# Last stage of a fused encoder: turning the normalised rows with transposing transfers on SyncE's queue instead of with TensorE

## The reference, cut to what matters

```python
h = einsum('bhid,oi,od->bho', x, weighted_sum, weight)      # mixing stage
h = concatenate([h, txt], axis=1)                           # 8 x 589 rows of 256
h = h + attn(layernorm(h))                                  # attention over the 8 rows of a position
h = h + ffn(layernorm(h))                                   # the last stage

def ffn(x):                                                 # x is layernorm(h)
    hn = rmsnorm(x, gamma1)                                 # "the normalised rows"
    q = hn @ Wq + bq
    kv = (hn @ Wdown + bdown) @ Wup + bup
    att = softmax(q k^T / 4) over the 16 heads of one row
    x = x + (att v) @ Wo + bo
    h2 = rmsnorm(x, gamma2)
    gate = softmax(h2 @ Wg + bg)                            # 8 experts
    return x + sum_e gate_e * (h2 @ We[e])
```

## Time and profile before

| | |
|---|---|
| median of 3 runs | 833.88 us (833.34 to 834.82) |
| profiled execution | 829.93 us, span 828.1 us |
| TensorE (PE) | 769.2 us busy, 93% |
| VectorE (DVE) | 729.4 us busy, 88% |
| ScalarE (ACT) | 335.1 us busy, 40% |
| GpSimd (POOL) | 405.2 us busy, 49% |
| mean granted clock of TensorE | 0.987 |

### The profile page before, as it was taken

The page is one execution under the profiler, slowest core; times in us unless marked ns, Lnnn a source line. Parts: engine busy times, 40 slices in busy tenths (PEclk is TensorE's granted clock), DMA queues, the critical chain, the costliest instruction groups (busy, mean ns, idle before and its releaser), DMA issues.

```text
span 828.1 us, 48492 instructions
## 1 busy us (share of the span) xinstructions
PE 769.2 (93%) x20348; PEld 512.0 (62%) x20348; DVE 729.4 (88%) x1702; ACT 335.1 (40%) x874; POOL 405.2 (49%) x1129
## 2 busy tenths in 40 slices
PE   4999978998998888986999999999999999999998
PEld 3888755665666666655666666666666656665654
DVE  5799678999999999975899999999999999999996
ACT  4577434444444444433333333333333333333321
POOL 1231355666665666743554455445545554554321
PEclk9999999999999999987999999999999999999999
DMA  9986000000000000000000000000000000000000
GB/s 329 340 213 217 1 3 4 1 0 0 0 0 0 0 0 0 4 4 4 11 10 15 13 13 6 13 13 13 6 13 13 13 6 13 13 6 13 14 16 19
DMA packets 17064, 28.38 MB, mean 34 GB/s; under 512 B 3474, under 2 KB 12258, under 8 KB 17002
## 3 DMA queue, kind: packets, MB, share of 16 engines
q1 hardware_dynamic: 17002, 27.49, 10.3%
HBM read 22.64 MB, written 4.83 MB: 33 GB/s over the span
## 4 chain that ended last, share of the span: by engine, by line
PE 62%; DVE 15%; issue 5%; ACT 3%; POOL 2%; DVEq 0%; ACTq 0%; POOLq 0%
PE bank L204 15%; PE bank L206 12%; PE bank L205 12%; PE bank L935 6%; PE bank L946 6%; DVE ss L462 3%; PE bank L287 3%; POOL rt L496 2%; PE bank L962 2%; DVE on_t_l L408 2%; PE bank L1004 2%; PE bank L953 2%; DVE k_t L459 1%; DVE sc L426 1%; DVE pr_t L439 1%
## 5 line engine op out<-in xcount | busy, mean ns | idle before, releaser
L1099 DVE SCALAR_TENSOR_TENSOR acc<-bank,gate,acc 128x256 f32<-128x256 f32 x222 | 105.3, 474 | 8.9 <-PE bank L206 2.5
L204 PE MATMUL bank<-we_h,h_t_h 128*128 128x512 f16 x296 | 113.0, 382 | 0.1
L206 PE MATMUL bank<-we_h,h_t_l 128*128 128x512 f16 x296 | 112.2, 379 | 0.0
L205 PE MATMUL bank<-we_l,h_t_h 128*128 128x512 f16 x296 | 112.2, 379 | 0.0
L204 PE MATMUL bank<-tokw_h,x_t_h 128*128 128x256 f16 x256 | 70.6, 276 | 11.7 <-DVE x_t_l L673 11.7
L206 PE MATMUL bank<-tokw_h,x_t_l 128*128 128x256 f16 x256 | 70.5, 275 | 0.0
L205 PE MATMUL bank<-tokw_l,x_t_h 128*128 128x256 f16 x256 | 70.5, 275 | 0.0
L946 PEld LDWEIGHTS bank<-pr_t,v 32*32 32x32 f32 x4736 | 48.1, 106 | 31.6 <-issue 31.6
L496 POOL TENSOR_TENSOR rt<-rn 128x32 f32<-128x32 f32 x111 | 26.5, 238 | 75.0 <-DVE rn L473 69.1
L935 PEld LDWEIGHTS bank<-kv_t,fq_t 32*32 32x32 f32 x4736 | 48.1, 106 | 18.8 <-issue 18.8
L375 ACT ACTIVATE pr<-sc 128x512 f32<-128x512 f32 x37 | 23.3, 630 | 87.8 <-DVE sc L426 87.8
(11 more groups left out here) (218 smaller groups left out, 2214.0 us busy)
## 6 DMA issues: line engine op xcount, KB each, us to landing
xbuf<-in_x SPq DMA_DIRECT2D x32, 512.0 KB, 5.4
out<-res SPq DMA_DIRECT2D x36, 128.0 KB
we_s<-in_we SPq DMA_DIRECT2D x4, 512.0 KB, 6.4
inw<-in_in_w SPq DMA_DIRECT2D x1, 768.0 KB, 11.0
wrep<-in_w_rep SPq DMA_DIRECT2D x1, 512.0 KB, 4.7
h_all<-in_txt SPq DMA_DIRECT2D x1, 512.0 KB
wst<-in_wst_in SPq DMA_DIRECT2D x1, 256.0 KB, 2.7
outw<-in_out_w SPq DMA_DIRECT2D x1, 256.0 KB, 11.0
```

What stands on the lines that cost most here:

```text
L204: nc.tensor.matmul(dst, a_h(c), b_h(c), start=start and c == 0, stop=False)
L205: nc.tensor.matmul(dst, a_h(c), b_l(c), start=False, stop=False)
L206: last = nc.tensor.matmul(dst, a_l(c), b_h(c), start=False, stop=stop and c == chunks - 1)
L1099: op = nc.vector.scalar_tensor_tensor(out=(res if e == E - 1 else acc)[:, :], in0=b_we[s % 2][:, k * D:(k + 1) * D], scalar=gate[p][:, e:e ...
```

## The change: what it does

The two transposes on TensorE, the copy to `hn_h` on ScalarE and the subtraction on VectorE go. ScalarE now writes the rows twice as they lie: `hn` in fp32 and, with the same operation, `hn_r[0]` in fp16. GpSimd subtracts the one from the other and writes `hn_r[1]` in fp16; the operation stands first in its part of a turn. Two transposing transfers of 128x256 fp16 elements each (64 KB), issued by SyncE, write `hn_h` and `hn_l` as before. They wait for the subtraction (`p_hnl`) and for the last reader of the tile before (`f_down`). TensorE waits for both to have landed (`hn_in`) before it multiplies with `wq`; ScalarE waits for the same before it writes the next tile's rows, because the transfers read `hn_r`. SyncE's loop is written out, with the transfers of tile `i` ahead of the output of tile `i - 4`.

```diff
@@ -821,6 +821,7 @@
         hn_h, hn_l = halves("hn_t", [P, KC, P])
+        hn_r = halves("hn_r", [P, D])
@@ ffn_pe
                 if real(i, 1):
-                    pe.wait_ge(f_htl, i + 2)
+                    pe.wait_ge(hn_in, 32 * (i + 2))
                     wait(pe, f_logit, i - 1)
                     rows_times(b_q[:, 0:D], hn_h, hn_l, ...
...
-                if real(i, 2):
-                    pe.wait_ge(f_hn, i + 3)
-                    wait(pe, f_x2, i)
-                    for c in range(KC):
-                        last = nc.tensor.transpose(b_hn[:, c * P:(c + 1) * P], hn[:, c * P:(c + 1) * P], ident[:, :])
-                    last.then_inc(f_hnps, 1)
@@ ffn_act
-                if real(i, 2):
-                    act.wait_ge(f_hnps, i + 3)
-                    wait(act, f_down, i + 2)
-                    nc.scalar.activation(hn_h[:, :, :], b_hn[:, 0:D], ACT.Copy).then_inc(f_hth, 1)
                 if real(i, 3):
                     settle(act, ls_ready)
-                    wait(act, f_hnps, i + 3)
+                    wait(act, p_hnl, i + 3)
+                    wait(act, hn_in, 32 * (i + 3))
                     act.wait_ge(p_all, i + 4)
                     at = bass.ds(i + 3, 1)
-                    nc.scalar.activation(hn[:, :], h_all[:, at, :].squeeze(1), ACT.Identity,
-                                         bias=..., scale=...).then_inc(f_hn, 1)
+                    for rows in (hn, hn_r[0]):
+                        last = nc.scalar.activation(rows[:, :], h_all[:, at, :].squeeze(1), ACT.Identity,
+                                                    bias=..., scale=...)
+                    last.then_inc(f_hn, 1)
@@ ffn_dve
-                if real(i, 2):
-                    dve.wait_ge(f_hth, i + 3)
-                    nc.vector.tensor_tensor(hn_l[:, :, :], b_hn[:, 0:D], hn_h[:, :, :], ALU.subtract).then_inc(f_htl, 1)
@@ ffn_pool
             def body(i, p):
+                if real(i, 2):
+                    pool.wait_ge(f_hn, i + 3)
+                    nc.gpsimd.tensor_tensor(hn_r[1][:, :], hn[:, :], hn_r[0][:, :], ALU.subtract).then_inc(p_hnl, 1)
@@ block.sync
-                with sp.Fori(0, TILES - 1) as i:
-                    sp.wait_ge(f_comb, (i + 1) * STEPS)
-                    sp.dma_start(out[bass.ds(i * P, P), :], res[:, :]).then_inc(out_done, 16)
-                sp.wait_ge(f_comb, TILES * STEPS)
-                sp.dma_start(out[(TILES - 1) * P:TOKENS, :], res[0:TAIL, :]).then_inc(out_done, 16)
+                for i in range(TILES + 4):
+                    if i < TILES:
+                        sp.wait_ge(p_hnl, i + 1)
+                        wait(sp, f_down, i)
+                        sp.dma_start_transpose(hn_h[:, :, :], hn_r[0][:, :]).then_inc(hn_in, 16)
+                        sp.dma_start_transpose(hn_l[:, :, :], hn_r[1][:, :]).then_inc(hn_in, 16)
+                    if i >= 4:
+                        at = (i - 4) * P
+                        rows = min(P, TOKENS - at)
+                        sp.wait_ge(f_comb, (i - 3) * STEPS)
+                        sp.dma_start(out[at:at + rows, :], res[0:rows, :]).then_inc(out_done, 16)
```

More of the change, by code:

```diff
@@ L902, in ffn_coefficients @@
             nc.gpsimd.tensor_copy(cf_all[:, at, :], cf[:, :].unsqueeze(1)).then_inc(p_all, 1)
-        names = ("f_hn", "f_hnps", "f_hth", "f_htl", "f_q", "f_down", "f_lat", "f_qraw", "f_qpad", "f_kv", "f_kvt", "f_qt",
+        names = ("f_hn", "p_hnl", "hn_in", "f_q", "f_down", "f_lat", "f_qraw", "f_qpad", "f_kv", "f_kvt", "f_qt",
                  "f_s", "f_max", "f_sub", "f_exp", "f_prt", "f_av", "f_of", "f_rsum", "f_on", "f_onps", "f_onh", "f_onl",
@@ L910, in build @@
                  "f_gmul", "f_we", "f_comb", "f_acc", "f_x1", "p_x1", "p_hx2", "p_t2", "p_r2", "p_latl", "out_done")
-        (f_hn, f_hnps, f_hth, f_htl, f_q, f_down, f_lat, f_qraw, f_qpad, f_kv, f_kvt, f_qt,
+        (f_hn, p_hnl, hn_in, f_q, f_down, f_lat, f_qraw, f_qpad, f_kv, f_kvt, f_qt,
          f_s, f_max, f_sub, f_exp, f_prt, f_av, f_of, f_rsum, f_on, f_onps, f_onh, f_onl,
@@ L1061, in body @@
                     nc.scalar.activation(h2_t[1 - p][0][:, :, :], b_turn[:, 0:D], ACT.Copy).then_inc(f_h2h, 1)
-                if real(i, 2):
-                    act.wait_ge(f_hnps, i + 3)
-                    wait(act, f_down, i + 2)
-                    nc.scalar.activation(hn_h[:, :, :], b_hn[:, 0:D], ACT.Copy).then_inc(f_hth, 1)
                 if real(i, 3):
                     settle(act, ls_ready)
-                    wait(act, f_hnps, i + 3)
+                    wait(act, p_hnl, i + 3)
+                    wait(act, hn_in, 32 * (i + 3))
                     act.wait_ge(p_all, i + 4)
                     at = bass.ds(i + 3, 1)
-                    nc.scalar.activation(hn[:, :], h_all[:, at, :].squeeze(1), ACT.Identity,
-                                         bias=cf_all[:, at, NR:NR + 1].squeeze(1),
-                                         scale=cf_all[:, at, RR:RR + 1].squeeze(1)).then_inc(f_hn, 1)
+                    for rows in (hn, hn_r[0]):
+                        last = nc.scalar.activation(rows[:, :], h_all[:, at, :].squeeze(1), ACT.Identity,
+                                                    bias=cf_all[:, at, NR:NR + 1].squeeze(1),
+                                                    scale=cf_all[:, at, RR:RR + 1].squeeze(1))
+                    last.then_inc(f_hn, 1)
                 if real(i, -1):
```

## The result

| | before | after |
|---|---|---|
| median of the runs made together, us | 833.61 (830.86 to 834.82, 4 runs) | 842.83 (840.86 to 843.95, 4 runs) |
| profiled execution, us | 829.93 | 842.81 |
| its span, us | 828.1 | 841.0 |
| mean granted clock | 0.987 | 0.971 |

The ratio is 1.011, with a 95% interval of 1.0083 to 1.0138. The change costs about 9 us.

A forecast was written before the change was run, and what follows sets the result against it. A loop between VectorE (`smax` to `h_t_l`) and TensorE (gate to scores) sets the 11.9 us turn. 829.93 + 9.2 - 1.7 = 837.4 profiled; with 3.95 to the median, 841.4; 8-in-10 range 835 to 848.

The forecast's parts named there:

- Loop, 0: Last stage, turns 3 to 34: removed work only lengthens TensorE's and VectorE's waits, turns stay 11.9 us; gain 0.
- Rival B: Last stage's loop: the removed work does set the pace, so not slower, 824.0 us or 828.0 as median; chance 0.07.
- L, 4.3: SyncE's queue: time from issue of the pair's first transposing transfer to the second's landing, taken as 4.3 us from `wu_b`.
- The stall, 9.2: Head turn -2: ScalarE waits for tile 0's late subtraction and transfers, delaying body 35's exponential; all 9.2 us lost.
- Rival C: Seam of the stages: stall half taken up, 836.8 us, chance 0.05; or no stall at all, 832.2, chance 0.05.
- The head gives back, -1.7: Head turns -1 to 2: removed transposes and VectorE work leave the path, 0.57, 0.5 and twice 0.3 us, together -1.7.
- clock, 0: TensorE's clock behind the stall: already at 0.50 there, so 0 us, with bounds of -0.5 and +2.5.

The follow-up runs named there:

- experiment 5: Changed kernel with equal unread work put back in the old places, two transposes on TensorE and a subtraction on VectorE: 842.9 us, ratio 1.0089.
- experiments 8 and 9: VectorE writes `h_t_l` earlier, reciprocal and one expert's combine behind it: 8 on the changed kernel with subtraction-first and two buffers, 821.49 us; 9 on the kernel before, 824.21.
- experiment 6: Changed kernel with three more transposing transfers ahead of the pair in each turn from tile 6 on: 845.82 us, ratio 1.0137.
- Experiments 1 to 3: Changed kernel with GpSimd's subtraction ahead of the attention body in head turns (1, 834.34 us), two buffers for `hn` and `hn_r` (2, 838.96), both (3, 833.43).
- experiment 3: Changed kernel with both the subtraction ahead of the attention body in head turns and two buffers for `hn` and `hn_r`: 833.43 us, ratio 1.0003.
- experiment 1: Changed kernel with GpSimd's subtraction ahead of the attention body in the head turns instead of behind it: 834.34 us, ratio 1.0014.

## Why the prediction was right

**The sign and the size** were right: 841.4 forecast, 842.83 measured, and most of it is the stall that the sum names. Two of the terms were off, in opposite senses.

**Loop, 0.** Right: turns of 11.90 and 11.91 us. The waits grew as the working had it: TensorE's for `h_t_l` from 13.1 to 17.9 us in 330, VectorE's before `smax` from 0.18 to 0.42 (forecast 0.6), and experiment 5 puts them back. Rival B, which the busy shares of 119 and 111 in 120 us spoke for, did not come true. What it had right is that something else must be removed first: with `h_t_l` earlier TensorE's work does set the pace (experiments 8 and 9).

**L, 4.3.** Measured 3.8, and experiment 6 shows that the loop has room to 7.5. The `wu_b` pair was a fair stand-in, for another reason than I gave: a transposing transfer holds the queue 1.17 to 1.28 us where `wu_b`'s first took 0.59, and lands sooner, 2.3 to 2.4 in place of 3.7. Of the two pages of the Trainium skill the trace bears out the second more nearly: "Advanced Engine Details and Errata", section "X-Bar Transpose (TRN2)", puts them on a par with ordinary transfers, and a 256 KB load landed in 2.7. That holds for the landing; the queue's time of 1.17 to 1.28 is well above the 0.33 to 0.35 of an output transfer. From the 1309 ns a block of the Trainium skill's "VectorE: DVE Perf Modes", section "The three transpose paths", I had made an estimate of 5.2 us for four blocks in turn; the pair took 3.8. The trace shows about the page's figure, 1.17 to 1.28, as the queue's time for a whole transfer of two blocks.

**The stall, 9.2.** It came where the chain put it, ended by the transfer it named, and was 8.60: 0.5 of the difference is L. Experiments 1 to 3 show its two causes, which are one chain: GpSimd's place for the subtraction (6.5 us of it) and the pair's own time. Rival C, no such stall, took experiments 1 and 3 to make by hand.

**The head gives back, -1.7, and clock, 0.** This step failed. Nothing was given back on balance; the head behind the stall cost 1.2 and 3.5 us in two executions. The transposes did leave the path, but little came of it even without a stall: from body 35's exponential to body 36's `smax`, where I had put 0.57, are 9.24 and 9.15 us before and 9.01 in experiment 3. In the changed kernel they are 9.48 both times: all of it runs at the low clock there, where before the granted clock was 0.69 in the mean. The rest was lost in later turns, at low stretches that before had elsewhere or not at all. How much of that the change brings stays open: experiment 5, with the removed work back, took 106.94 us to the eighth `smax`, between the changed kernel's 105.28 and 107.51, and two executions of one kernel differ by as much as the term. I had given the clock bounds of -0.5 to +2.5 and taken 0, since the stretch behind the stall "ran at 0.50 already"; that was true of 364.0 to 369.3 and again from 376, not between them. (The 1.6 us of 4 that I gave for TensorE ahead of it is 360 to 364, when the clock had already fallen; in the 4 us before the fall, 358.4 to 362.4, it was busy 2.2.) In the kernel before the clock was full again from 369.5 to 375.5 (first row below); in the changed one TensorE was busy 7.2 of 16 us from 366 on, and the whole of body 36 and then 13 us of turns 0 and 1 ran at 1.2 GHz (the second trace):

```profile
369.50:375.50 6.00, 4.47 (x271) 3.53 (x267) 4.20 (x9) 1.22 (x3) 0.72 (x1) 1.00 0.02 5
```

```profile
366.00:382.00 16.00, 7.24 (x87) 4.56 (x87) 5.99 (x11) 4.45 (x11) 3.70 (x6) 0.50 0.09 18
389.50:402.50 13.00, 12.06 (x411) 8.58 (x412) 7.85 (x16) 3.12 (x9) 5.52 (x14) 0.50 0.04 9
```

The errors have opposite signs but do not cancel: the stall is 0.6 too large, what follows 2.9 to 5.2 too small by the profiled executions. Over the runs the excess is smaller: the medians of the runs made together differ by 9.2 (6.9 to 11.5 by the interval), against 7.5 in my sum. That 841.4 came within 1.4 us is in part luck: a second execution of the same kernel moves the head alone by that much, and the sum rests on 3.95 us between one profiled execution and the median, while in the changed kernel the two agree (842.81 and 842.83).

## What to carry to other kernels

Two engines that are each 90% busy or more can still wait for each other once a turn, and then work taken from either is worth nothing until the instruction that closes the loop comes earlier; here moving that one gave 10 to 12 us, and on top of it the removal gave some 2 by the length of the turns, which the timed runs cannot tell from nothing. When a step passes from one engine to a chain of three (ScalarE, GpSimd, a queue), look at the seam between stages, where each engine's list has an old stage's work in front of the new step: one subtraction of 0.66 us in the wrong place cost 6.5 us. Two buffers without the earlier start only hand the wait to the next reader.

## What the hardware showed that I had not expected

- Transposing transfers of 128x256 fp16 out of SBUF into SBUF don't overlap in their issue: 1.17 to 1.28 us of the queue each, five in 6.33 and three in 3.74. A single one near the seam could take longer, 1.73 in experiment 1, 2.02 in 3 and 2.13 in 2.
- They land 2.3 to 2.4 us after their issue whether two or seven stand in a row, and the loop's engines didn't slow down beside 39.4 MB of traffic in place of 33.3: 11.91 us a turn with three extra in each.
- Keeping TensorE busy in a stall of 9 us did keep its clock (0.86 in place of 0.72 over 62 us), and yet it was no gain: the low stretches came later instead, at 385, 395 and 409 us, and the timed runs were slower than without.
- The same program had 17.1 us of low clock in its head in one execution and 27.3 in the next, for 1.5 us of time.
